# Cross attention: the LayerNorm variance one step later, the second half of the output projection two steps behind the first, the last half in the query bank

## The reference, cut to what matters

```
h = layernorm(x);  x = attention(h, h) + x        # self attention
h = layernorm(x);  x = attention(h, context) + x  # cross attention
h = layernorm(x);  x = feed_forward(h) + x
```

```
q = h @ wq ; k = context @ wk ; v = context @ wv
p = softmax(scale * q k^T)          # over the 64 context positions
x = concat_heads(p v) @ wo + bo + x
```

## Time and profile before

| quantity | value |
|---|---|
| median of 3 runs | 5385.88 us (5373.51 to 5387.13) |
| the profiled execution | 5388.29 us, its span 5386.5 us |
| granted TensorE clock, mean | 0.957 |
| busy share of the span | PE 91%, DVE 73%, ACT 44%, POOL 48% |
| cross attention, first layer | about 3017 to 3190 us |
| cross attention, second layer | about 3956 to 4171 us |
| cross attention, third layer | about 4993 to 5210 us |

### The profile page before, as it was taken

The page is one execution under the profiler, slowest core; times in us unless marked ns, Lnnn a source line. Parts: engine busy times, 40 slices in busy tenths (PEclk is TensorE's granted clock), DMA queues, the critical chain, the costliest instruction groups (busy, mean ns, idle before and its releaser), DMA issues.

```text
span 5386.5 us, 53903 instructions
## 1 busy us (share of the span) xinstructions
PE 4888.6 (91%) x18976; PEld 2662.3 (49%) x18976; DVE 3938.4 (73%) x3854; ACT 2377.5 (44%) x4086; POOL 2609.8 (48%) x1336
## 2 busy tenths in 40 slices
PE   7888988888888888877999889999998999999999
PEld 4455555555555555543555444555544445554444
DVE  4999999999999999985777653666645246665641
ACT  5555555555556555533434333433333233333321
POOL 2555555555555555555777112766600046665000
PEclk8999999999999999898999999999999999999999
DMA  2434343443343443430000010000001000001000
GB/s 106 143 143 147 132 152 144 146 147 143 143 147 145 140 143 144 151 126 13 1 1 24 16 39 1 1 1 1 24 24 38 3 1 1 1 1 48 0 1 16
DMA packets 94249, 376.65 MB, mean 70 GB/s; under 512 B 12960, under 2 KB 14240, under 8 KB 91040
## 3 DMA queue, kind: packets, MB, share of 16 engines
q1 hardware_dynamic: 93984, 373.19, 19.2%
HBM read 369.87 MB, written 3.28 MB: 69 GB/s over the span
## 4 chain that ended last, share of the span: by engine, by line
PE 45%; DVE 6%; ACT 1%; issue 1%; POOL 1%; DVEq 0%; ACTq 0%; POOLq 0%
PE PS L1141 6%; PE PS L1165 6%; PE PS L1151 6%; PE PS L1120 6%; PE PS L1328 5%; PE PS L1339 3%; PE PS L1129 3%; PE PS L1175 3%; PE PS L1288 2%; PE PS L1252 1%; PE PS L1240 1%; DVE PA L1670 1%; DVE CST L1668 1%; POOL PA L1086 1%; PE PS L1107 1%
## 5 line engine op out<-in xcount | busy, mean ns | idle before, releaser
L645 POOL TENSOR_TENSOR UH<-UH,BC 128x1152 f32<-128x1152 f32 x512 | 1344.5, 2626 | 1062.0 <-DVE U L714 1062.0
L1086 POOL TENSOR_SCALAR PA<-PA,INV 128x512 f32<-128x512 f32 x768 | 1190.9, 1570 | 595.8 <-DVE INV L1584 595.8
L392 PE MATMUL Y<-UH,ident_sb 128*128 128x512 f32 (+1 forms) x3072 | 1170.5, 526 | 240.9 <-POOL UH L645 135.9
L722 DVE TENSOR_TENSOR_SCAN UH<-DA,U 128x1152 f32<-128x1152 f32 x512 | 1307.2, 2553 | 21.7 <-ACT DA L583 4.3
L392 PEld LDWEIGHTS Y<-UH,ident_sb 128*128 128x128 f32 x3072 | 588.1, 203 | 863.2 <-issue 570.5
L1399 ACT ACTIVATE PA<-PS,NMX 128x512 f32<-128x512 f32 x768 | 519.4, 684 | 726.8 <-DVE NMX L1578 554.6
L583 ACT ACTIVATE DA<-DT,NEGA 128x575 f32<-128x575 f32 x1024 | 718.7, 763 | 101.1 <-DVE UH L722 69.8
L714 DVE TENSOR_TENSOR U<-DTX,BC 128x1152 f32<-128x1152 f32 x512 | 699.2, 1366 | 55.8 <-DVE DTX L700 7.1
L1593 DVE COPY VP<-PS 128x512 f32<-128x512 f32 x768 | 494.7, 685 | 280.3 <-PE PS L1151 259.1
L1578 DVE TENSOR_REDUCE NMX<-PS 128x2 f32<-128x1024 f32 x384 | 452.3, 1218 | 51.5 <-PE PS L1141 51.2
L1151 PEld LDWEIGHTS PS<-ident_sb,PA 128*128 128x128 f32 x3072 | 352.4, 142 | 241.4 <-issue 196.4
(11 more groups left out here) (157 smaller groups left out, 5419.8 us busy)
## 6 DMA issues: line engine op xcount, KB each, us to landing
BC<-bc_rows SPq DMA_DIRECT2D x512, 576.0 KB, 3.6
ARENA<-mamba_a SPq DMA_DIRECT2D x16, 1421.0 KB, 7.3
ARENA<-pair_w SPq DMA_DIRECT2D x6, 3072.0 KB, 10.5
WB<-mamba_b SPq DMA_DIRECT2D x16, 514.0 KB, 5.0
VP<-ff_w SPq DMA_DIRECT2D x2, 3072.0 KB
WO<-out_w SPq DMA_DIRECT2D x4, 1024.0 KB
stream<-x_t SPq DMA_DIRECT2D x2, 1024.0 KB, 10.2
VP<-ff_w SPq DMA_DIRECT2D x2, 1024.0 KB
```

What stands on the lines that cost most here:

```text
L392: mm = pe.matmul(Y[:, a:b], IDENT[:, :], UH[:, SLOT[j], a:b], start=(s == 0), stop=(s == DS - 1), skip_group_check=True)
L645: pool.tensor_tensor(h, h, BC[:, j % NBB, 1, :].unsqueeze(1).broadcast_to([P, HK, T]), ALU.mult).then_inc(s_hc, 1)
L722: dve.tensor_tensor_scan(UH[:, SLOT[j], :], DA[:, j % NDA, :], U[:, 0:HC], 0.0, ALU.mult, ALU.add).then_inc(s_scan, 1)
L1086: pool.tensor_scalar(PR[:, n % 3, j, :], PR[:, n % 3, j, :], INV[:, n % 4, j:j + 1], None, ALU.mult).then_inc(s_ps, 1)
```

## The change

The second half of the output projection moves from step 13 to step 14 (and correspondingly 22 and 30), its add from 14 to 15. The LayerNorm jobs move so that `mean` is in step 16, 24, 32. In every job, the one at M = 2 too, `variance` and `deviation` come three steps behind `mean`, and `norm` four. The loop is one step longer. The last half, `finish(3, 1)`, goes to bank 0 and no longer waits for `add(3, 0)`, but until DVE has taken the last query product out of bank 0. No instruction is added or removed, except waits.

```diff
 def cross_norms(l):
     at = {2: job(l, 1, NB - 1)}
-    at.update({NP * (b + 1) + 7: job(l, 2, b) for b in range(NB - 1)})
+    at.update({NP * (b + 2): job(l, 2, b) for b in range(NB - 1)})
     return at

                     def finish(b, m):                                   # PE
                         i = b * KD + m
-                        pe.wait_ge(s_x, START + l * XADD + NB * KD + i)
+                        bank = 0 if i == NB * KD - 1 else 1
+                        pe.wait_ge(s_x, START + l * XADD + NB * KD + i - (1 if bank == 0 else 0))
+                        if bank == 0:
+                            pe.wait_ge(s_cqr, START + TBASE[l + 1])
...
-                            mm = pe.matmul(PS[:, 1, :], ...)
+                            mm = pe.matmul(PS[:, bank, :], ...)

-                    for at in range(NITS + 4):
+                    for at in range(NITS + 5):
...
-                        if 0 <= at - 4:
+                        if 0 <= at - 4 < NITS:
                             values(at - 4)
-                        if NP + 4 <= at < NITS and at % NP in (4, 5):
-                            finish(at // NP - 1, at % NP - 4)
+                        if NP + 4 <= at < NITS and at % NP in (4, 6):
+                            finish(at // NP - 1, at % NP // 2 - 2)
                         if at in CN_AT[l]:
                             mean(CN_AT[l][at], 1)
-                        if at - 2 in CN_AT[l]:
-                            pe.wait_ge(s_cent, START + CN_AT[l][at - 2] + 1)
-                            variance(CN_AT[l][at - 2], 1)
+                        if at - 3 in CN_AT[l]:
+                            pe.wait_ge(s_cent, START + CN_AT[l][at - 3] + 1)
+                            variance(CN_AT[l][at - 3], 1)

-                        if at - 2 in CN_AT[l]:                          # ACT
-                            deviation(CN_AT[l][at - 2], 1)
+                        if at - 3 in CN_AT[l]:
+                            deviation(CN_AT[l][at - 3], 1)

-                        if NP + 5 <= at < NITS and at % NP in (5, 6):   # DVE
-                            add(at // NP - 1, at % NP - 5)
+                        if NP + 5 <= at < NITS and at % NP in (5, 7):
+                            add(at // NP - 1, at % NP // 2 - 2)
...
-                        if at - 3 in CN_AT[l]:
-                            norm(CN_AT[l][at - 3])
+                        if at - 4 in CN_AT[l]:
+                            norm(CN_AT[l][at - 4])
```

More of the change, by code:

```diff
@@ L1287, in finish @@
                         for t in range(NTL[l]):
-                            mm = pe.matmul(PS[:, 1, :], wo[:, t, m * P:(m + 1) * P], ATT[:, (b * NTL[l] + t) % NAT, :],
+                            mm = pe.matmul(PS[:, bank, :], wo[:, t, m * P:(m + 1) * P], ATT[:, (b * NTL[l] + t) % NAT, :],
                                            start=(t == 0), stop=(t == NTL[l] - 1))
@@ L1469, in output @@
                                        bias=VEC[:, l % 2, c:c + 1]).then_inc(s_ca, 1)
-                    for at in range(NITS + 4):
+                    for at in range(NITS + 5):
                         if 0 <= at - 3 < NITS:
                             turned(at - 3)
-                        if at >= 4 and (at - 4) % PPT[l] == PPT[l] - 1:
+                        if 0 <= at - 4 < NITS and (at - 4) % PPT[l] == PPT[l] - 1:
                             output(at - 4)
@@ L1686, in add @@
                         dve.wait_ge(s_op, START + l * NB * KD + b * KD + m + 1)
-                        dve.scalar_tensor_tensor(out=xv[:, m, b, :], in0=PS[:, 1, :], scalar=VEC[:, l % 2, c:c + 1],
+                        bank = 0 if (b, m) == (NB - 1, KD - 1) else 1
+                        dve.scalar_tensor_tensor(out=xv[:, m, b, :], in0=PS[:, bank, :], scalar=VEC[:, l % 2, c:c + 1],
                                                  in1=xv[:, m, b, :], op0=ALU.add, op1=ALU.add).then_inc(s_x, 1)
-                    for at in range(NITS + 4):
+                    for at in range(NITS + 5):
                         if 0 <= at - 2 < NITS:
```

## The result

| | before | changed |
|---|---|---|
| median of 4 runs each, on one chip | 5386.51 us (5373.51 to 5388.62) | 5343.66 us (5334.53 to 5345.38) |
| second measurement (17 and 5 runs) | 5386.01 us | 5346.05 us (5329.35 to 5348.99) |
| cross attention, first / second / third layer | 173.06 / 215.07 / 216.74 us | 154.09 / 204.15 / 204.14 us |
| the three together | 604.87 us | 562.38 us |
| span less these three | 4781.6 us | 4770.3 us; 4781.8 in the second measurement |

The ratio of the first measurement is 0.9922 (95% interval 0.9905 to 0.9938), of the second 0.9916 (0.9902 to 0.993). The forecast was 5347 us, 3.3 us above the first measurement and 1 us above the second. The runs of one kernel lie in groups some 10 us apart (the kernel before at 5374 to 5380 and at 5384 to 5389), so a median of a few runs can move by as much without the change having a part in it.

What follows compares the result with a forecast made beforehand. DVE's loop sets the first layer's pace, PE bounds the second and third. Gains 10.2 + 12.8 + 0.8 + 4.9 + 4.2 + 3.2 = 36.1 us plus 3 of clock make 39: median 5347 us, range 5335 to 5370.

Steps and rivals of the forecast that it cites:

- (a): PE's `finish(b, 1)` waits for `add(b, 0)` behind `shift` on DVE: 2.02 us in first layer, 1.31 in second.
- (b): PE's `variance` waits for `centre`, squares and POOL's add: 2.94 us in first layer, 0.96 in second.
- (c): PE's query waits for DVE's query behind `norm`: 1.23 us.
- the job at M = 2: LayerNorm job at M = 2: late scores cost 0.84 us in first layer, nothing in the others; gain 0.8.
- first layer, two periods: Eight-step periods, old 39.8 and 41.4 us, each to become 34.7: gain 10.2, plus 1.6 if the clock drop goes.
- second and third layer, four periods: Eight-step periods of 50.94 us to become 47.75, with PE waiting 0.8 for a query: gain 12.8.
- ends: `finish(3, 0)` starts earlier: 4.9 us for second and third layer together, 4.2 for first, with 0.9 put to the clock.
- clock taken: Lower-clock losses of 1.6, 0.9 and 1.65 us in three stretches, together 4.1; 3 of it counted as gain.
- 1 (waits move to DVE, 5358): Scores late by 3.44 us instead of 0.7, query wait 1.4 instead of 0.8: 10.5 less gain; chance 0.15.
- 2 (the inner waits hidden, 5374): Inner waits were hidden anyway and only the end counts, 12.3 us; chance 0.12.
- 4 (clock drops stay): Clock drops stay at the end, where PE idles between short bursts: 3 us less, 5350; chance 0.15.
- 3 (one step too late): `deviation` behind `exps` on ACT slips a DVE step, PE waits before every `finish(b, 0)`: 5396 us; chance 0.05.

Runs made afterwards that it cites:

- the variance alone: Kernel before, with only `variance` and `deviation` moved to three steps behind `mean` and `norm` to four: 5364.45 us, ratio 0.9969.
- the spacing alone: Changed kernel with everything in bank 1 and `variance`, `deviation`, `norm` as early after `mean` as before: 5366.44 us, ratio 0.9959.
- the first two experiments: The spacing alone (5366.44 us, ratio 0.9959) and the variance alone (5364.45 us, ratio 0.9969).

## Why the prediction was right, point by point

The mechanism came as forecast: the waits (a), (b) and (c) gone or as small as counted, the periods within 0.25 us, the ends within 0.1 us. The misses are small, and three make most of the 3.5 us by which the gain exceeded the 39: 1.1 of clock, 1.0 for the job at M = 2, 1.0 in the periods of the second and third layer.

**Where the time came from.** From the three cross attentions, 42.5 us (18.97, 10.92 and 12.6). Forecast were 39 with the clock. The median fell by 42.9, and by 40.0 in the second measurement.

**Term by term** (gain in us):

| term | forecast | measured |
|---|---|---|
| first layer, two periods | 10.2, and 1.6 of clock | 11.9 |
| second and third layer, four periods | 12.8 | 13.8 |
| job at M = 2 | 0.8 | 1.8 |
| ends | 4.9 and 4.2, and 2.55 of clock | 11.7 |
| last half in bank 0 | 3.2 | 3.3 |
| clock taken | 3 of the 4.1 above | no drop left |
| sum | 39 | 42.5 |

**First layer.** The count of DVE's loop gave a period of 34.7; it was 34.58 and 34.67. The scores after the second half-projection were to be late by 0.7; they were by 0.68. The wait on `deviation` was put at 0.65; it is 0.15 and 0.16 in the two periods. A slip in the count did no harm: `centre`, 1.21 against 0.70 of idle time, adds 0.5 and not 0.4. The experiment with the variance alone adds a caution: in this layer part of a wait that is taken away, 1.3 of 2.9, comes back in the next one.

**Second and third layer.** Forecast 47.75, measured 47.51. I took 3.98 of waits off the old period; no row shows that figure (the rows have 3.5 of idle time, and my own subtraction gave 4.2), but it was right, since the measured period less its one wait is 46.95. The 0.24 is that wait, PE's for a query: I had 0.8, and this row of the changed kernel, second layer, has 0.56.

```profile
4067.74 1.96 PE L1252 MATMUL PS<-HN,ARENA 128*128 128x512 f32 x4 [0.56 <-DVE PA L1660]
```

**The job at M = 2.** I said that DVE bounds these steps in the second and third layer and put nothing. They gained 0.43 and 0.44. This is a small miss of the step itself: I had read the late scores in the first layer alone. The 0.94 of the first layer is near the 0.84, but that can be chance. Its stretch had a lower clock in the kernel before, which I had not read and which is no part of the 4.1; it is at 1.00 in the changed kernel. How much of the 0.94 is the scores and how much the clock no run separates. Busy time by stretch, kernel before:

```profile
3017.55:3066.83 49.28, 41.34 (x187) 24.80 (x186) 38.68 (x65) 16.48 (x28) 2.77 (x2) 0.97 0.00 1
```

**The ends.** `finish(3, 0)` was to start 28.4 us after `finish(2, 0)` in the first layer, and 38.78 in the others; it was 28.50 and 38.72. The first layer's end gained 4.99, and 4.2 with 0.9 of clock is 5.1; how it divides between the two is not shown.

**The clock.** The term that was mis-sized. I took 3 us of 4.1 because two rows with such waits showed no drop. I said that three of five such waits were in a stretch with a drop; with the one in the stretch above (2.81 us ahead of `variance`) it was four of six. In cross attention no drop is left in either profile of the change: its longest wait is 1.80. That such a drop comes of waits is supported by all twelve profiles: the clock fell 30 times in cross attention, each time during a wait of PE of 1.95 us or more or within 1 us behind it, and not once at the shorter waits. But the length of one wait doesn't settle it, for there were 47 waits of that length. With the spacing alone a wait of 1.96 passed without a drop and one of 1.95, one period later, was followed by slower matmuls (the transposes at 3130.27 took 1.06 in place of 0.60) and a period 1.65 longer at 0.95; and the 3.70 of the earlier trace rows had none. What decides in a single case stays open.

**What I missed.** I wrote that POOL's clearing "is through before the last add", and did not ask what it does to DVE while it runs. It makes PE wait 3.5 us longer in each of the first two experiments and costs the whole change nothing, by luck: the bank of the last half had taken the only reader of that delay away. With the banks exchanged it came back, in part.

**A sign that was put badly.** I had named as a sign of being wrong that the half-projection waits for `deviation` by more than a microsecond. It does, 1.49 before `finish(3, 0)` in each layer. But the forecast itself counts this wait, as the "about 1.6" that is the longest one left; the sign holds only for the halves of the other entries, and there it is 0.16 at most.

**The rivals.** 1 (waits move to DVE, 5358): fell; 0.68 and 0.56 are the small waits of the forecast. 2 (the inner waits hidden, 5374): fell; the periods gained 25.7, the ends 11.7. 4 (clock drops stay): fell. 3 (one step too late) did not happen. Its price in PE's waits was about right per place, but its total for one whole step was to be 49 with the clock; an experiment that is one step late only in `deviation`, with the waits 3.05 and 4.54 instead of my 3.4 and 5.0, gave 39. DVE's own wait in `norm`, and with it the job at M = 2, was not in it.

## What to carry to other kernels

Work through a pipelined loop engine by engine, in starts and not in busy time, and look for instructions that wait for something of the same step; one step more of distance makes such a wait vanish where the engine has other work, and one step more on the wrong side costs nearly as much as it gained. Price a change with all of its parts together, and compare by stretch: the parts here make 36.3 us and the whole 42.4, but that is 7.9 too much in the periods, where two parts take away the same wait, and 11.2 too little at one end, where one part hides a delay that the others bring. When two elementwise engines start to overlap in a new way, compare the duration of each instruction with its row from before, before you look for a wait.

## What the runs showed of the hardware

**A tensor_scalar on VectorE and a memset on GpSimd exclude each other.** Two tensor_scalars of 128x512 f32, SBUF to SBUF, take 0.87 to 0.88 us together; beside GpSimd's memsets of 128x4096 f32 (3.51 us each) they took 4.63, 6.85 and 7.25, and where they got in between two memsets, the second had 3.79. Moving the memsets brought them to 0.87 again. It is not so for every VectorE instruction: in the changed kernel the two scalar_tensor_tensors of `norm` run beside the same memset (3149.54 to 3153.05) and take 1.41 together, where they take 1.40 without it. The Trainium skill ("SBUF — State Buffer", section "Who interferes with whom") says that a VectorE instruction such as tensor_scalar can enter a mode that takes a port pair shared with GpSimd, and that then whoever comes first holds it for the whole instruction. These rows agree, with a GpSimd instruction that only writes.

**The granted clock after a wait.** PE was at 1.00 over all of cross attention in the changed kernel, with waits up to 1.80; in the kernel with the late `deviation` it was at 0.97 over the period with waits of about 3 us shown above, that is some of its time at 1.2 GHz instead of 2.4. The Trainium skill ("TensorE: Matmul & The Clock Gate", section "HAM oscillation — how this bites in real kernels") says that pauses between bursts of matmuls throttle the engine again, each time anew; the runs agree for most of the long waits and not for all: 30 drops at 47 waits of 1.95 us or more, and 3.70 us passed without one.
